# Mixture of experts in two passes: one scattered row and one result row for each token

## The reference, cut to what matters

```python
# x: 32 graphs x 256 nodes x 128 channels, adj: 0/1 with 6% ones, 16 experts of 128 -> 256 -> 128
h = layernorm(x) @ W.T + b
att = sigmoid((h @ a1)[:, :, None] + (h @ a2)[:, None, :] + att_b) * adj     # and the node mask
x = x + (att / (sum(att) + 1e-8)) @ h
t = layernorm(x)                                          # 8192 tokens
topk_vals, topk_idx = top_k(t @ gate_w + gate_b, 2)       # two experts for each token
topk_w = softmax(topk_vals)
expert_out = relu(t @ w1[e] + b1[e]) @ w2[e] + b2[e]
y = t + sum(topk_w * expert_out of the two chosen experts)
x = x + layernorm(y) * gamma + beta
```

## Time and profile before

| | us |
|---|---|
| median of three runs (456.19 to 458.34) | 456.4 |
| the profiled execution: its own time | 456.47 |
| its span in the profile | 454.7 |
| PE busy in the span | 343.6 (76%) |
| DVE busy | 295.3 (65%) |
| ACT busy | 228.1 (50%) |
| POOL busy | 303.0 (67%) |

### The profile page before, as it was taken

The page is one execution under the profiler, slowest core; times in us unless marked ns, Lnnn a source line. Parts: engine busy times, 40 slices in busy tenths (PEclk is TensorE's granted clock), DMA queues, the critical chain, the costliest instruction groups (busy, mean ns, idle before and its releaser), DMA issues.

```text
span 454.7 us, 11203 instructions
## 1 busy us (share of the span) xinstructions
PE 343.6 (76%) x2287; PEld 279.0 (61%) x2287; DVE 295.3 (65%) x1466; ACT 228.1 (50%) x704; POOL 303.0 (67%) x331
## 2 busy tenths in 40 slices
PE   4688878877878854200998988988888889888992
PEld 3566767766767753100897777777777778833330
DVE  4687899999999884610476666666555555610664
ACT  3568869978999844100333333333333334311662
POOL 5620767777777777773277777777777777771565
PEclk9999989999999985555799999999999999999998
DMA  7812536645555643496866777777777776316994
GB/s 239 282 59 71 170 137 190 184 162 163 165 174 199 212 151 107 160 234 216 256 184 186 213 218 205 237 211 217 212 222 217 214 232 191 108 37 239 391 347 138
DMA packets 61683, 88.10 MB, mean 194 GB/s; under 512 B 10213, under 2 KB 40859, under 8 KB 61490
## 3 DMA queue, kind: packets, MB, share of 16 engines
q1 hardware_dynamic: 30786, 43.45, 32.5%
q0 software_dynamic: 10720, 25.32, 15.7%
q10 hardware_dynamic: 20112, 18.63, 13.8%
HBM read 55.61 MB, written 32.73 MB: 194 GB/s over the span
## 4 chain that ended last, share of the span: by engine, by line
PE 25%; DVE 20%; issue 13%; DMA 12%; POOL 12%; ACT 5%; ACTq 2%; DVEq 1%; POOLq 1%; SPq 0%
POOL token_y L445 8%; DMA token_y<-yb,xb 5%; PE psum L1265 5%; PE psum L1254 5%; DMA xb<-sorted_x 4%; POOL sorted_x L422 3%; ACT xn L535 3%; PE psum L1167 3%; PE psum L1298 2%; PE psum L1299 2%; DVE i L848 2%; PE psum L1157 2%; DMA out_dram<-xrow 1%; PE psum L1139 1%; DVE newton L812 1%
## 5 line engine op out<-in xcount | busy, mean ns | idle before, releaser
L445 POOL DMA_INDIRECT token_y<-yb,xb x143 | 143.3, 1002 | 58.1 <-issue 35.4
L422 POOL DMA_INDIRECT sorted_x<-xrow,rows x128 | 123.5, 964 | 60.1 <-issue 56.8
L606 ACT ACTIVATE hid<-psum,b_sb 128x256 f32<-128x256 f32 (+1 forms) x188 | 69.2, 419 | 142.7 <-PE psum L1254 72.0
L1265 PE MATMUL psum<-w_sb,hid 128*128 x572 | 83.1, 282 | 7.0 <-ACT hid L606 5.7
L1265 PEld LDWEIGHTS psum<-w_sb,hid 128*128 128x128 f32 x572 | 75.0, 192 | 15.5 <-issue 12.9
L1254 PE MATMUL psum<-xbT,w_sb 128*128 128x256 f32 (+1 forms) x376 | 81.7, 341 | 2.4 <-DVE xbT L1025 2.2
L1034 DVE TENSOR_TENSOR yb<-psum,b_bc 128x256 f32<-128x256 f32 (+1 forms) x94 | 33.9, 360 | 63.0 <-PE psum L1265 59.4
L1254 PEld LDWEIGHTS psum<-xbT,w_sb 128*128 128x128 f32 x376 | 58.2, 194 | 8.3 <-DVE xbT L1025 5.2
L1244 PE MATMUL psum<-ident_aug,xb 128*128 128x128 f32 x143 | 33.5, 292 | 29.6 <-DMA xb<-sorted_x 27.2
L1025 DVE COPY xbT<-psum 128x256 f32<-128x256 f32 (+1 forms) x94 | 33.2, 354 | 23.6 <-PE psum L1244 23.3
L1039 DVE SCALAR_TENSOR_TENSOR yb<-yb,xb 128x128 f32<-128x128 f32 x143 | 46.1, 351 | 3.3
(11 more groups left out here) (168 smaller groups left out, 567.6 us busy)
## 6 DMA issues: line engine op xcount, KB each, us to landing
xb<-sorted_x SPq DMA_DIRECT2D x49, 258.0 KB, 3.1
w_sb<-w_dram ACTq DMA_DIRECT2D x94, 128.0 KB, 2.9
adj_in<-adj_dram SPq DMA_DIRECT2D x32, 256.0 KB
got<-token_y SPq DMA_DIRECT2D x16, 512.0 KB, 5.7
xb<-sorted_x SPq DMA_DIRECT2D x45, 129.0 KB, 2.8
out_dram<-xrow ACTq DMA_DIRECT2D x16, 256.0 KB, 3.4
xmid<-x_dram SPq DMA_DIRECT2D x6, 512.0 KB, 8.0
token_y<-yb,xb POOLq DMA_INDIRECT x143
```

Source lines behind the costliest of these rows:

```text
L422: pool.indirect_dma_start(sorted_x, bass.IndirectOffsetOnAxis(ap=rows[:, slot, t, k:k + 1], axis=0), xrow[:, slot, k, t, :], None).then_in ...
L445: pool.indirect_dma_start(token_y, bass.IndirectOffsetOnAxis(ap=xb[:, q, t, TO:TO + 1].bitcast(I32), axis=0), yb[:, h, t, :], None, bounds ...
L606: last = act.activation(hid[:, u % RING, c, 0:n], psum[:, 2 + u % 2, c * BT:c * BT + n], ACT.Relu, bias=b1_sb[:, c, e])
L1265: last = mm(psum[:, 4 + u % 2, t * D:(t + 1) * D], hid[:, u % RING, c, t * P:(t + 1) * P], w2_sb[:, e, c * D:(c + 1) * D].rearrange("p a c ...
```

## The change

The 16 lists become two sets of 16: one for the first choice of each token, one for the second. A token's row is scattered once, to its first expert's list (`sorted1`, 134 columns: x, the result's row, the row in either list, both weights). The experts then run in two passes. In the first, the result tile is written in place beside x, and `send` scatters the whole row of 262 columns to the second expert's list (`sorted2`). In the second, the expert's result is added to the first and one row of 128 columns goes to `token_y`. Each pass has room for 17 blocks and 45 tails of one set of lists: 79 tiles, 158 in all. The tails after the first go two to a unit, each with an expert, a row load and a w1 load of its own: 40 units in a pass (one tail, 17 blocks, 22 pairs of tails). The second pass's first load waits until the first pass's sends have all landed, and the input ring has 8 slots in place of 11.

The Newton chain leaves DVE: POOL works out 1/sqrt of both layernorms with a power instruction (`rstd1_of`, `rstd2_of`), between its scatters. ACT writes the normalised rows straight into `xrow`, so `keep`'s copies go, and `xrow` has four slots in place of three. The padding of the first lists is shared by SP (six), ACT (five) and POOL (five, behind its scatters); that of the second lists is done by SP within the first pass. In the last stage there is nothing to add: ACT and DVE read the loaded rows directly, and PE has no part in it. The table is computed for both sets at once; its rows tell nothing more and are left out.

```diff
-FULL = (ITEMS - EXPERTS * (BT - 1)) // BT + 1
-TAILS = (ITEMS - FULL * BT) // P + EXPERTS - 1
-IN_RING = 11
+LISTS = TOPK
+FULL = (TOKENS - EXPERTS * (BT - 1)) // BT + 1
+TAILS = (TOKENS - FULL * BT) // P + EXPERTS - 1
+UNITS = ((FULL,),) + tuple((b,) for b in range(FULL)) + tuple(
+    (FULL + i, FULL + i + 1) for i in range(1, TAILS, 2))
+IN_RING = 8
...
-SCATTERS = TPP * TOPK
+SCATTERS = TPP
+SP_FILLS, ACT_FILLS = range(0, 6), range(6, 11)
+POOL_FILLS = range(11, EXPERTS)
...
+        def load_w1(engine, l, u):
+            q = u % IN_RING
+            for t, b in enumerate(UNITS[u]):
+                engine.dma_start(w1_sb[:, q, t, :], w1[expert_of(engine, l, b), :, :].rearrange("e a c -> a (e c)")
+                                 ).then_inc(w1_in[q], 16)
...
+            sp.wait_ge(filled[0], 16 * (len(SP_FILLS) + len(ACT_FILLS) + 1))
+            sp.wait_ge(filled_by_pool, 16 * len(POOL_FILLS))
...
+            for u in range(len(UNITS)):
+                load_unit(0, u)
+                if IN_RING <= u + 1 < IN_RING + EXPERTS:
+                    fill(sp, 1, u + 1 - IN_RING)
+            sp.wait_ge(filled[1], 16 * (EXPERTS + 1))
+            for q in range(IN_RING):
+                sp.wait_ge(unit_out[q], 16 * sent(last_in(q), 0))
+            sp.sem_inc(sp_passed, 1)
+            for u in range(len(UNITS)):
+                load_unit(1, u)
...
-            for i in range(PAIRS):
-                turn(i, i % XROWS)
...
+            for m in range(4, PAIRS + 2):
+                if m <= PAIRS:
+                    rstd2_of(m - 1)
+                scatter(m - 2)
+                if m in (6, 7):
+                    rstd1_of(m + 1)
+            pool.wait_ge(fill_done, 1)
+            for e in POOL_FILLS:
+                fill(g, 0, e, [filled_by_pool])
...
+                    if l == 0:
+                        pool.indirect_dma_start(
+                            sorted2, bass.IndirectOffsetOnAxis(ap=xb[:, q, t, D + ROW2:D + ROW2 + 1].bitcast(I32), axis=0),
+                            xb[:, q, t, :], None, bounds_check=PAD_ROW - 1, oob_is_err=False).then_inc(unit_out[q], 16)
+                    else:
+                        pool.indirect_dma_start(
+                            token_y, bass.IndirectOffsetOnAxis(ap=xb[:, q, t, D + TO:D + TO + 1].bitcast(I32), axis=0),
+                            xb[:, q, t, 0:D], None, bounds_check=TOKENS - 1, oob_is_err=False).then_inc(unit_out[q], 16)
...
-                act.copy(xrow[:, slot, 1, :, 0:D], xn2[:, :, :])
-                act.copy(xrow[:, slot, 0, :, 0:2 * D].rearrange("p t (a c) -> p t a c", c=D),
-                         xn2[:, :, None, :].broadcast_to([P, TPP, 2, D])).then_inc(x_kept, 1)
...
+                experts = [expert_of(act, l, b) for b in UNITS[u]]
...
+                for t, e in enumerate(experts):
+                    for c in range(FC):
+                        last = act.activation(hid[:, v % RING, c, t * P:t * P + n], psum[:, 2 + v % 2, c * BT + t * P:c * BT + t * P + n],
+                                              ACT.Relu, bias=b1_sb[:, c, e])
...
-                r = variance(m - 1, graphs(m, 1) if valid(m) else ())
-                norm_route_and_place(r, m - 2)
+                variance(m - 1, graphs(m, 1) if valid(m) else ())
+                route(m - 2)
+                place_pair(m - 2)
...
-                mm(y_v, ident[:, :], got[:, q, :, 0, :], start=True, stop=False)
-                mm(y_v, ident[:, :], got[:, q, :, 1, :], start=False, stop=True).then_inc(summed, 1)
```

More of the change, by code:

```diff
@@ L332, in _ @@
             sp.dma_start(b2_bc[:, :, :], b2_even.partition_broadcast(P)).then_inc(b2_in, 16)
-            sp.dma_start(sorted_x[PAD_ROW:PAD_ROW + P, :], pad_rows[:, :]).then_inc(filled, 16)
+            sp.wait_ge(const_done, CONSTS)
+            sp.dma_start(sorted1[PAD_ROW:PAD_ROW + P, :], pad_rows[:, D:RW2]).then_inc(filled[0], 16)
+            sp.dma_start(sorted2[PAD_ROW:PAD_ROW + P, :], pad_rows[:, :]).then_inc(filled[1], 16)
             sp.wait_ge(fill_done, 1)
-            for e in range(0, EXPERTS, 2):
-                row = sp.value_load(fill_row[0:1, e:e + 1], min_val=0, max_val=PAD_ROW - P)
-                sp.dma_start(sorted_x[bass.ds(row, P), :], pad_rows[:, :]).then_inc(filled, 16)
+            for e in SP_FILLS:
+                fill(sp, 0, e)
@@ L436, in _ @@
-            for i in range(PAIRS):
-                turn(i, i % XROWS)
-            def send(u):
-                q, h = u % IN_RING, u % OUT_RING
-                pool.wait_ge(yb_done, u + 1)
+            rstd2_of(0)
+            rstd1_of(5)
+            rstd2_of(1)
+            scatter(0)
+            rstd2_of(2)
+            scatter(1)
+            rstd1_of(6)
+            for m in range(4, PAIRS + 2):
[4 more added lines that the diff above has]
+                    rstd1_of(m + 1)
@@ L453, in finish @@
+            for l in range(LISTS):
+                for u in range(len(UNITS)):
+                    send(l, u)
             def finish(i):
@@ L499, in weigh @@
                 act.wait_ge(chosen_done, i + 1)
-                for k in range(TOPK):
-                    last = act.activation(xrow[:, slot, k, :, WEIGHT], lead[:, :], ACT.Sigmoid, scale=1.0 - 2.0 * k)
+                act.copy(xrow[:, slot, :, TO].bitcast(I32), result_row[:, i * TPP:(i + 1) * TPP])
+                for k, column in enumerate((WEIGHT1, WEIGHT2)):
+                    last = act.activation(xrow[:, slot, :, column], lead[:, :], ACT.Sigmoid, scale=1.0 - 2.0 * k)
                 last.then_inc(xrow_done, 1)
@@ L1306, in _ @@
[L1306 to L1311 removed]
+            for l in range(LISTS):
+                e1 = e2 = None
+                for u in range(len(UNITS) + 2):
+                    e0 = [expert_of(pe, l, b) for b in UNITS[u]] if u < len(UNITS) else None
+                    if u < len(UNITS):
+                        turn_x(l, u)
+                    if 1 <= u <= len(UNITS):
+                        layer1(l, u - 1)
+                    if u >= 2:
+                        layer2(l, u - 2, e2)
+                    e1, e2 = e0, e1
```

659 lines of the change are left out of this document (291 added, 368 removed).

## The result

The changed kernel takes 510.6 us (median of 4 runs, 509.72 to 514.25), the kernel before 456.7 in the same comparison: 1.1205 times as long, 95% interval 1.1148 to 1.1261. The profiled execution has a span of 509.3 us. I had said 486, with a range up to 506: slower is what came, but by 24.8 us more of span than the sum of 484.5, and the time lies outside the range.

The account below looks back on a forecast made before the run. POOL's scatters and sends were taken as the bound, with ACT's queue just as full in the expert stage. 454.7 - 16.4 - 10.2 + 59.9 - 3.5 = 484.5, plus 1.8 outside the span: 486 us, range 452 to 506.

Parts of the forecast that it names:

- The sign and the mechanism of the passes: Expert stage: ACT's register reads and loads set the pairs of tails, making the stage 59.9 us longer; slower overall, chance 0.82.
- my 99.6: Expert stage, both passes: 14 pairs of tails a pass at ACT's 3.56 us each, 49.8 us a pass.
- My own bound of 3.9: Expert stage: upper bound in us for a pair with two loads, if the relus hold ACT's reads up.
- the idle 1.08 us: Kernel before, expert stage: ACT's idle time without a shown wait, between a block and the next tail; taken as a full queue.
- The rival that POOL alone bounds the passes: Expert stage: ACT's reads overlap its relus and POOL's sends decide, 101.9 us a pass, 452.7 us in all; chance 0.18.
- The clock rival: Expert stage: PE's clock falls in the pairs, a pair takes 4.4 us, 23.5 us more, 510 in all; chance 0.13.
- The last stage: After the last send: earlier squares save 2 us and sooner stores 1.5; shorter by 3.5, to 40.3, bounds 0 and 8.
- The graph stage: Up to the copy into `fill_row`: an ordinary turn falls 0.8 us to 7.9; shorter by 16.4 in all.
- a rival with a turn of 8.74: Graph stage: `rstd2_of` behind the scatters is as late as the old chain, 16.4 us come back, 503; chance 0.11.
- Borders: From `fill_row` to the first row load: fewer POOL arrears, 14.6 us against 24.8, shorter by 10.2.
- The hole between the passes: Expert stage: POOL stands between the last send of one pass and the first of the next, 12.2 us.
- the 8.6: Ramp from the first row load to the first send, 8.6 us, taken from the kernel before.

Follow-up runs that it names:

- the run with kept registers: Kernel before, with ACT keeping the register of a w1 load for that unit's relu, one of two reads fewer: 457.7 us, ratio 1.0040.
- the split: Changed kernel with two of each pair's four graph-stage scatters moved behind the next pair's `rstd2_of`: 500.8 us, ratio to before 1.0971.
- with kept registers: Changed kernel with ACT reusing each w1 load's register for that tile's relu, two of a pair's four reads fewer: 478.9 us, ratio to before 1.0488.
- the three edits: Changed kernel with ACT's registers kept, gamma copied to PSUM and the graph stage's scatters split around `rstd2_of`: 457.2 us, ratio to before 1.0034.

## Why the prediction was wrong

**The sign and the mechanism of the passes were right.** The pairs came at the pace of ACT's sequencer, with POOL waiting. The term was mis-sized: where I had 3.56 us a pair, the rows above have 3.84, and by the starts of POOL's sends the 14 pairs took 54.2 us in the first pass and 52.4 in the second, 3.81 each, 7.1 us more than my 99.6 and most of the 10.5. Beside them the first ten units of the two passes took 2.9 more, the last eight pairs 2.1 more and the eight blocks ahead of the pairs 1.5 less. My own bound of 3.9, for relus that hold the reads up, was the nearer end. But the ground I gave was false. I read the idle 1.08 us of the earlier trace rows as the proof of a second full queue; in the kernel before nothing hung on it, as the run with kept registers shows. It became the bound only because a pair has two loads and four reads.

**The rival that POOL alone bounds the passes** asked that a pair cost ACT under 2.58. It cost 3.84, so the rival fell; with two reads gone the kernel is nearly that rival, with passes of 111.4 and 106.1 against its 101.9.

**The clock rival named a time, 510, that came, by a mechanism that did not.** PE's granted clock in stretches made mostly of pairs (length, busy us of PE, PEld, DVE, ACT and POOL, clock, DMA share, GB/s):

```profile
260.00:300.00 40.00, 25.71 (x188) 22.04 (x188) 18.29 (x57) 11.44 (x40) 21.21 (x22) 1.00 0.58 170
380.00:420.00 40.00, 26.09 (x193) 22.39 (x191) 15.03 (x52) 11.64 (x41) 22.92 (x24) 1.00 0.65 186
```

PE was busy for 64% and 65% of the time and its clock was full, 2.4 GHz. The rule of the Trainium skill that I weighed (Perfetto Trace Analysis, section Matmul Optimizations) would have cost the 23.5 us priced there; this trace does not bear it out at that share.

**The last stage failed in the bounds.** I had priced what the change takes away there, two matmuls and half the bytes, and gave the gain bounds of 0 and 8 without a reason that excluded a loss. The scale's input moved from PSUM to SBUF and I costed that at nothing, though `finish` on POOL runs beside it in every group. With one operand back in PSUM the stage takes 38.0, so the gains that I forecast (40.3) were there: the miss is the lock, 10.3 us, less 2.3 that I had left out. A loss of 4.5 (48.3 against 43.8) for the bound of 0 would have carried the range from 506 to 510.5, to the edge of the measured time.

**The graph stage failed in one step.** I set POOL's 7.0 us of work beside a turn of 7.9 and took it to fit. What counts is when `rstd2_of` can begin: the scatters start only when the rows are placed, late in the turn, and it stands behind 5.05 us of them. DVE's last instruction of the placing, the first of the four scatters and the first instruction of `rstd2_of` in one turn:

```profile
127.36 0.29 DVE L821 TENSOR_REDUCE xrow<-picked 128x8 int32<-128x128 f32 x1
128.46 1.08 POOL L489 DMA_INDIRECT sorted<-xrow  x1 [1.41 <-issue]
133.43 0.24 POOL L476 TENSOR_SCALAR var<-mv 128x4 f32<-128x4 f32 x1
```

`norm2` of that turn follows at 135.41. I had named that as a rival with a turn of 8.74; ordinary turns took 8.1 where I had 7.9, so it held in part; the last turn took 10.2 (159.34 to 169.52) and `norm2` waited 2.15 in it, and with the split the stage ends earlier (166.0) than I had forecast. That ACT's copies were "not last" I had read from the long turns: in the ordinary ones of the earlier trace rows `norm2` began with no wait. Some of the 7.0 belongs to this one execution: four other kernels with the same graph stage copy to `fill_row` at 174.8 to 175.9. In the changed kernel's profile PE's clock had fallen, in this stretch:

```profile
65.00:72.00 7.00, 7.00 (x33) 6.47 (x32) 2.59 (x21) 5.99 (x18) 4.20 (x7) 0.55 0.17 57
```

That is nearly the lower level, 1.2 GHz, after PE had been busy for 2.85 of the 5 us ahead (60 to 65), and one turn took 11.05 us (71.05 to 82.10, in the rows of `norm2`), the same one 8.7 with kept registers. With kept registers, a nearly equal 3.05 of those 5 us was followed by the full clock. Why it fell in the one and not in the other stays open.

**Borders.** The hole between the passes was right (12.3 for 12.2). POOL's fills cost 0.7 each, not 1.26, which gave 2.8 back; small waits took 0.4 of that. The ramp was 1.6 longer, and PE in order of time shows where, first before, then in the changed kernel:

```profile
214.58 0.47 PE L1244 MATMUL psum<-ident_aug,xb 128*128 128x128 f32 x1 [19.41 <-DMA xb<-sorted_x]
...
217.35 1.22 PE L1254 MATMUL psum<-xbT,w_sb 128*128 128x128 f32 x4 [0.38 <-DVE xbT L1025]
218.37 1.06 PE L1265 MATMUL psum<-w_sb,hid 128*128 x4
```

```profile
192.72 0.48 PE L1247 MATMUL psum<-ident_aug,xb 128*128 128x128 f32 x1 [5.67 <-DMA xb<-sorted]
194.40 0.69 PE L1247 MATMUL psum<-ident_aug,xb 128*128 128x128 f32 x2 [1.20 <-DMA xb<-sorted]
...
196.26 1.92 PE L1258 MATMUL psum<-xbT,w_sb 128*128 128x256 f32 x4
197.97 1.00 PE L1270 MATMUL psum<-w_sb,hid 128*128 x4
```

The first tail's layer 2 (last row of each) begins 3.79 us after the first transpose before, and 5.25 now: 1.46 of the 1.6. The second unit was a tail and is now a block, and PE transposes it ahead of the first tail's layer 1: it waits 1.20 for the block's rows, and the block's layer 1 of 1.92 comes next. I had carried the 8.6 over without looking at the order of the first units. No run changed that order alone, so this is read from the rows and not shown. With ACT's burst of w1 loads cut to three the ramp was 10.2 us against 10.8 with the three edits.

## What to carry to other kernels

- Idle time that ends with "issue" shows a sequencer at work, not a bound: look at what is late next before it is priced, and keep a register in place of a second read where the sequencer does set the pace.
- When an operand moves from PSUM to SBUF, look at what the engine beside it does at that moment, even if the instruction itself stays the same.
- Work that is handed to another engine costs its place in that engine's queue, not its share of the engine's time: set its start, not its length, against the turn. And where a gain bounded by zero has no row that excludes a loss, carry the loss into the range.

## What had not been expected of the hardware

Four 128x128 scales on DVE took 1.14 us alone, 2.16 beside POOL's add of 1.26 us when both of a scale's tensors lay in SBUF, and 1.12 beside it with one of the two in PSUM. A plain DMA of 128 rows issued by POOL took it about 0.7 us with its gap, an indirect one 1.26 to 1.29 with its gap. In an ACT queue full of loads and reads, two reads or one load with its read were worth the same: taking either away brought a pair of the second pass from 3.75 us to 2.65 on the mean, near POOL's 2.58.
